# Stacking copies of q and k issued on GpSimd's queue or on SP's: one core, a macaron layer

## The chip, the cores and the metric

The kernel runs on one core of one Trainium2 chip. The metric is the device time of one execution in microseconds. The kernel before was timed three times: 2951.03, 2951.1 and 2961.06 us, median 2951.1 us.

## The reference

A layer of three parts with residual connections, on `x` of 16 sequences x 512 tokens x 128 values, float32:

```
x = x + 0.5 * ffn(layernorm(x))
x = x + attn(layernorm(x))
x = x + 0.5 * ffn(layernorm(x))
```

`ffn` routes each token to 2 of 8 experts (gate = sigmoid of the router's score) and adds a shared expert; each expert is `(silu(x W_in) * (x W_gate)) W_out`, 128 -> 256 -> 128. The change is in `attn`: 16 heads of 8 values,

```
scores = (q k^T + einsum('bhqd,qkd->bhqk', q, rel_emb[clip(i - j, -128, 128) + 128])) / sqrt(8)
local  = softmax(scores) v
global = (sigma M) / (sigma z + 1e-6),   sigma = elu(q) + 1
out    = (gate * local + (1 - gate) * global) Wo^T + bo
```

with `q, k, v = x W^T + b` and `gate = sigmoid(gate_alpha)`.

## The kernel before, in words

X stays in SBUF for the whole kernel. `ffn_phase` runs twice, `attention_phase` between them. Float32 products are made exact enough by splitting an operand into a high and a low part (`q_hi = round(q)`, `q_lo = q - q_hi`).

The attention goes over 128 items: 16 sequences x 4 sets of 4 heads (`set_of`) x 2 halves of the 512 queries (`half_of`). The program of each engine is written out as a list of slots, `for c in SLOTS: slot(c)`, one slot per item, eight (`PER`) per sequence, and each slot has four groups `k`. In slot `c` PE does the transposed scores of item `c`, the plain scores of item `c + 2` (for the row maxima), the relative products of item `c + 4` (`band_product`, L768), and parts of the preparation of the coming sequence and of the output of the leaving one. `(2, 0)` below is slot 2 of the eight, group or half 0.

The relative term takes a way through DRAM. PE multiplies the stacked queries with the table of relative embeddings into `ps_r` (L768, one buffer); ACT copies it to `src` (`at_src`, L904, `band_out_of_psum`), for which it first waits until the band write of the item before has landed and so freed that half of `src`; POOL (`send_band`) adds a column of padding (L952, L953) and writes it to `at_band` in DRAM (L959); SP (`fetch_rel`, L1027) reads it back with a skewed stride, so that the diagonals become rows, into `rel`; POOL's `fill_far` (L969) fills the part beyond distance 128. DVE then adds `rel` to the plain scores and takes the row maxima (L1089), one item ahead PE turns these (L797), DVE copies them to `mrow` (L1099), and SP copies `mrow` into a row of the stacked queries `qs` (`maxima_in`, L1036), so that the transposed scores have the maximum subtracted by the product itself. PE waits for that copy at the first group of a slot (`scores_turned`, L730).

The stacked operands `qs` and `ks` hold, for each head of a set, three parts on 24 partitions: `q_hi, q_hi, q_lo` against `k_hi, k_lo, k_hi`. Each of the 12 pieces of `qs` and of the 12 of `ks` is a copy of its own within SBUF (`spread`, L1044): 32 partitions x 2 KB onto 8 partitions x 8 KB, 64 KB. They are issued four at a time at the six places `QUERIES_IN` (2,0), (2,1), (3,0) and `KEYS_IN` (3,1), (4,0), (4,1). The queries are needed by `band_product` from (4,0) on, for the coming sequence.

On SP the order in a slot is: fetch of `rel` half 0 of item `c + 3` (four DMAs), the maxima of item `c + 1`, four stack copies where the place has them, fetch of half 1, four stack copies. On POOL: `send_band(c + 3, 1)`, `fill_far(c + 3)`, `send_band(c + 4, 0)`, then `project`: `q_lo` in slot 1, `k_lo` in slot 2 (L977, L980), three operations for sigma and the bias in slot 3 (L983, L986, L988), one in slot 4 (L993); and in slot 3 the sum of the two outputs (L1007).

Of the kernel before, what the change touches and what calls it, by code (L numbers as in the profile page):

```python
# [6 lines left out]
F32, F32R, BF16, U32 = mybir.dt.float32, mybir.dt.float32r, mybir.dt.bfloat16, mybir.dt.uint32  # L7
# [522 lines left out]
def attention_phase(nc, io, X, STATS, tables):  # L530

    D = X.shape[2]
    H, HD = io["head_of"].shape[1], io["M"].shape[1]
# [4 lines left out]
    HG = 4  # L538
    SETS = H // HG
    PART = 3  # L540
    ROW = PART * HD
    HALF = 2 * P
    PER = 2 * SETS
# [7 lines left out]
    R2 = 2  # L551
# [6 lines left out]
    QUERIES_IN = ((2, 0), (2, 1), (3, 0))  # L558
    KEYS_IN = ((3, 1), (4, 0), (4, 1))

    with ExitStack() as ctx:
# [19 lines left out]
        q_hi, q_lo = sb("q_hi", [P, S], F32R), sb("q_lo", [P, S], F32R)  # L581
        k_hi, k_lo = sb("k_hi", [P, S], F32R), sb("k_lo", [P, S], F32R)
# [72 lines left out]
        q_in = [ring(f"q_in{r}", 16 * PART * HG) for r in range(R2)]  # L655
# [20 lines left out]
        def item(c):  # L676

            return c if 0 <= c < ITEMS else None

        def coming(c):  # L680

            b = c // PER + 1
            return b if 0 <= b < B else None
# [261 lines left out]
        @block.gpsimd  # L945
        def _(pool):
            def send_band(c, l):

                j = c
                pool.wait_ge(qr_out.sem, qr_out.at(j, 2 * l + 2))  # L950
                edge = src[:, l, :, BAND - 1:BAND]
                pool.tensor_copy(far[:, c % RREL, l], edge).then_inc(pad_done.sem, 1)  # L952
                pool.tensor_copy(src[:, l, :, BAND:WIDE], edge.broadcast_to([P, HG, PAD])).then_inc(pad_done.sem, 1)  # L953
                if item(c - 2) is not None:
                    r_ring, n = rel_ring(c - 2, l)
                    pool.wait_ge(r_ring.sem, r_ring.at(n, 64))
                pool.wait_ge(pad_done.sem, pad_done.at(j, 2 * l + 2))
                heads = band.ap()[(2 * c + l) % 4].rearrange("p (h e) -> p h e", h=HG)
                pool.dma_start(heads[:, :, PAD:HEADW], src[:, l]).then_inc(band_out[l].sem, 16)  # L959

            def fill_far(c):

                j = c
                t_done.wait(pool, j, -3 * 2 * HG)
                pool.wait_ge(pad_done.sem, pad_done.at(j, 4))
                for l in range(2):
                    key = P * (2 * half_of(c) + l - 1) + WIDE + 1
                    if key < S:
                        pool.tensor_copy(rel[:, c % RREL, l, :, key:S],  # L969
                                         far[:, c % RREL, l].broadcast_to([P, HG, S - key])).then_inc(fill_done.sem, 1)  # L970

            def project(c):

                b, r, place = coming(c), 1 - par_of(c), c % PER
                if place == 1:
                    pool.wait_ge(qhi_done.sem, qhi_done.at(b, 1))
                    pool.tensor_tensor(q_lo[:], q32[:], q_hi[:].bitcast(F32), ALU.subtract).then_inc(qlo_done.sem, 1)  # L977
                elif place == 2:
                    pool.wait_ge(khi_done.sem, khi_done.at(b, 1))
                    pool.tensor_tensor(k_lo[:], k32[:], k_hi[:].bitcast(F32), ALU.subtract).then_inc(klo_done.sem, 1)  # L980
                elif place == 3:
                    g_prod.wait(pool, b, -2)
                    pool.tensor_scalar(sigma[:, r, :], q32[:], 0.0, None, ALU.min).then_inc(neg_done.sem, 1)  # L983
                    pool.wait_ge(neg_done.sem, neg_done.at(b, 1))
                    pool.wait_ge(xn_done.sem, xn_done.at(b, 1))
                    pool.tensor_scalar(q32[:], q32[:], 0.0, None, ALU.max).then_inc(pos_done.sem, 1)  # L986
                    rows = X[:, bass.ds(b * QPB, QPB), :]
                    pool.tensor_tensor(rows, rows, bo[:].rearrange("p (t d) -> p t d", t=1).broadcast_to([P, QPB, D]),  # L988
                                       ALU.add).then_inc(bo_done.sem, 1)
                elif place == 4:  # L990
                    pool.wait_ge(neg_exp.sem, neg_exp.at(b, 1))
                    pool.wait_ge(pos_done.sem, pos_done.at(b, 1))
                    pool.tensor_tensor(sigma[:, r, :], sigma[:, r, :], q32[:], ALU.add).then_inc(sigma_done.sem, 1)  # L993

            def slot(c):
                if item(c + 3) is not None:
                    send_band(c + 3, 1)
                    fill_far(c + 3)
                if item(c + 4) is not None:
                    send_band(c + 4, 0)  # L1000
                if coming(c) is not None:
                    project(c)
                if leaving(c) is not None and c % PER == 3:
                    b = leaving(c)
                    pool.wait_ge(o_step.sem, o_step.at(b, 2 * QPB))
                    pool.wait_ge(g_step.sem, g_step.at(b, 6))
                    pool.tensor_tensor(glob[:], glob[:], local[:], ALU.add).then_inc(mixed_done.sem, 1)  # L1007
            for c in SLOTS:
                slot(c)

        @block.sync
        def _(sp):
            def fetch_rel(c, l):

                j, qb = c, 2 * half_of(c) + l
                sp.wait_ge(band_out[l].sem, band_out[l].at(j, 16))
                n = j // 2
                sp.wait_ge(fill_done.sem, fill_done.at(n, l + 1 if half_of(c) == 0 else 3))
                max_done.wait(sp, j, 4 * (l + 1) - 2 * 2 * HG)
                r_ring, n = rel_ring(c, l)  # L1020
                for g in range(4):
                    first = P - 1 - 32 * g if qb == 0 else 0
                    last = BAND - 1 - 32 * g if qb == QPB - 1 else WIDE
                    key = P * (qb - 1) + 32 * g + 1 + first
                    row = ((2 * c + l) % 4 * P + 32 * g) * PITCH
                    rows = bass.AP(band, row + PAD + first, [[PITCH - 1, 32], [HEADW, HG], [1, last - first]])
                    sp.dma_start(rel[32 * g:32 * g + 32, c % RREL, l, :, key:key + last - first], rows).then_inc(r_ring.sem, 16)  # L1027

            def maxima_in(c):

                j = c
                sp.wait_ge(m_row.sem, m_row.at(j, 1))
                m_ring, n = pair_ring(m_in, c)
                at = (ROW * R2 + par_of(c)) * SETS * S + set_of(c) * S + HALF * half_of(c)
                to = bass.AP(qs[:].tensor, at, [[32 * R2 * SETS * S, HG], [1, HALF]])
                sp.dma_start(to.bitcast(F32), mrow[:, c % R2, :].bitcast(F32)).then_inc(m_ring.sem, 16)  # L1036

            def spread(c, b, n, parts, to, rings):

                r = b % R2  # L1040
                for m in range(HG * n, HG * n + HG):
                    h, a = divmod(m, PART)
                    at = 32 * h + HD * a
                    sp.dma_start(to[at:at + HD, r].bitcast(F32), parts[a][32 * h:32 * h + 32, :].bitcast(F32)).then_inc(rings[r].sem, 16)  # L1044

            def stack(c, half):

                b, place = coming(c), (c % PER, half)
                if place in QUERIES_IN:
                    n = QUERIES_IN.index(place)  # L1050
                    if n == 0:
                        sp.wait_ge(qlo_done.sem, qlo_done.at(b, 1))
                        t_done.wait(sp, c - c % PER, 0)
                    spread(c, b, n, (q_hi, q_hi, q_lo), qs, q_in)
                elif place in KEYS_IN:
                    n = KEYS_IN.index(place)
                    if n == 0:
                        sp.wait_ge(klo_done.sem, klo_done.at(b, 1))
                    spread(c, b, n, (k_hi, k_lo, k_hi), ks, k_in)

            def slot(c):
                if item(c + 3) is not None:
                    fetch_rel(c + 3, 0)
                if item(c + 1) is not None:
                    maxima_in(c + 1)
                if coming(c) is not None:
                    stack(c, 0)
                if item(c + 3) is not None:
                    fetch_rel(c + 3, 1)
                if coming(c) is not None:  # L1070
                    stack(c, 1)
            for c in SLOTS:
                slot(c)

# [332 lines left out]
```

## Time and profile before

| | |
|---|---|
| median of 3 runs | 2951.1 us |
| profiled execution, its own time | 2947.33 us |
| its span | 2945.5 us |
| TensorE clock granted, mean | 0.961 |
| PE busy | 2752.1 us (93%) |
| DVE / ACT / POOL busy | 1893.1 / 1735.6 / 1392.2 us (64 / 59 / 47%) |

Lines beginning with an engine are instructions or groups of them; `SPq` and `POOLq` are DMAs issued by SP and by GpSimd (POOL). A DMA's duration is that of its issue; its landing is separate. Busy digits are tenths of a slice of span / 40, here 73.6 us.

### The profile page before, as it was taken

What the parts mean: (1) busy time and instruction counts of PE and PEld (TensorE: products, weight loads), DVE (VectorE), ACT (ScalarE), POOL (GpSimd) and SP (SyncE); (2) the same over time, 40 slices, a digit from 0 to 9 for tenths busy, and PEclk for the clock granted to TensorE, in tenths of its full rate; (3) what the DMA queues carried; (4) which work ended last, traced back from release to release, by engine and by line L of the source; (5) the groups of instructions that cost most, each with busy time, mean ns of one, the idle gap of its engine ahead of it and who ended that gap; (6) DMA issues with size and microseconds to landing.
All of it is one profiled execution on the core that took longest, in us unless ns stands there. A gap on an engine that the chain in (4) does not pass through costs nothing. (4 is left out here: it accounts for less than half of the span.)

```text
span 2945.5 us, 60238 instructions
## 1 busy us (share of the span) xinstructions
PE 2752.1 (93%) x18624; PEld 1985.9 (67%) x18624; DVE 1893.1 (64%) x4781; ACT 1735.6 (59%) x3222; POOL 1392.2 (47%) x1728
## 2 busy tenths in 40 slices
PE   5999999999499999999999999999998999999999
PEld 4777777777255666566666565666656777777777
DVE  7666666667256666666666666666647666666665
ACT  4656566655256666556666555666646656665655
POOL 3555555555444344444434444444414555555554
PEclk9999999999689999999999999999998999999999
DMA  4000000000377788888878877887831000000000
GB/s 115 1 0 0 0 0 0 0 0 1 66 220 221 223 235 230 213 219 224 226 219 224 225 213 215 229 224 228 230 103 50 8 7 4 7 7 4 7 6 9
DMA packets 233801, 324.94 MB, mean 110 GB/s; under 512 B 29444, under 2 KB 188548, under 8 KB 233604
## 3 DMA queue, kind: packets, MB, share of 16 engines
q1 hardware_dynamic: 194436, 171.36, 24.5%
q0 software_dynamic: 36864, 150.49, 15.3%
q8 instruction: 106, 1.74, 0.3%
q10 hardware_dynamic: 2304, 0.61, 0.1%
q14 instruction: 91, 0.75, 0.1%
HBM read 141.68 MB, written 154.92 MB: 101 GB/s over the span
## 5 line engine op out<-in xcount | busy, mean ns | idle before, releaser
L1089 DVE CUSTOM_DVE_ANT_0 at_junk<-at_ps_s,at_rel 128x512 bf16<-128x512 f32 x1024 | 666.1, 688 | 403.9 <-PE at_ps_s L758 386.3
L895 ACT ACTIVATE at_probs<-at_ps_t 128x512 f32<-128x512 f32 x1024 | 558.7, 595 | 504.5 <-PE at_ps_t L743 504.3
L378 POOL TENSOR_TENSOR ffn_h_lo<-ffn_h,ffn_h_hi 128x512 fp32r<-128x512 f32 x384 | 502.1, 1311 | 475.6 <-ACT ffn_h_hi L305 475.6
L489 DVE TENSOR_TENSOR ffn_h<-ffn_silu,ffn_ps_gate 128x512 f32<-128x512 f32 x576 | 393.7, 683 | 406.7 <-ACT ffn_silu L348 404.4
L305 ACT CAST ffn_h_hi<-ffn_h 128x512 fp32r<-128x512 f32 x576 | 358.8, 623 | 408.4 <-DVE ffn_h L489 407.0
L194 PE MATMUL ffn_ps_mid<-ffn_xT_hi,ffn_w_mid 128*128 128x512 f32 x1152 | 480.2, 417 | 22.7 <-DVE ffn_h L489 11.5
L743 PE MATMUL at_ps_t<-tab_ident,at_rel 128*128 128x128 f32 x3328 | 497.1, 290 | 0.0
L194 PE MATMUL ffn_ps_gate<-ffn_xT_hi,ffn_w_gate 128*128 128x512 f32 x1152 | 456.7, 396 | 0.0
L194 PE MATMUL ffn_ps_out<-ffn_h_hi,ffn_w_out 128*128 128x512 f32 x1152 | 453.9, 395 | 0.2
L743 PEld LDWEIGHTS at_ps_t<-tab_ident,at_rel 128*128 128x128 f32 x3328 | 372.2, 146 | 82.3 <-issue 22.7
L348 ACT ACTIVATE ffn_silu<-ffn_ps_mid 128x512 f32<-128x512 f32 x576 | 343.8, 597 | 80.2 <-PE ffn_ps_gate L194 73.2
L372 POOL TENSOR_TENSOR ffn_xe<-ffn_xn,ffn_gate 128x512 f32<-128x512 f32 x256 | 269.3, 1057 | 238.6 <-DVE ffn_gate L451 124.4
L730 PEld LDWEIGHTS at_ps_t<-at_qs,at_ks 25*128 25x128 f32 x2048 | 189.7, 188 | 281.7 <-ACT at_probs L895 126.4
L730 PE MATMUL at_ps_t<-at_qs,at_ks 25*128 25x256 f32 x2048 | 300.7, 335 | 55.3 <-DMA at_qs<-at_mrow 55.0
L904 ACT COPY at_src<-at_ps_r 128x512 f32<-128x512 f32 x512 | 304.3, 594 | 65.0 <-PE at_ps_r L768 38.2
L783 PE MATMUL at_ps_v<-at_probs,at_v 128*32 128x256 f32 x4096 | 337.8, 403 | 0.2 <-ACT at_probs L895 0.2
L952 POOL COPY at_far<-at_src 128x4 f32<-128x4 f32 x256 | 48.2, 188 | 606.2 <-ACT at_src L904 603.7
L768 PE MATMUL at_ps_r<-tab_rs,at_qs 128*128 128x512 f32 x512 | 260.6, 509 | 36.6 <-DMA at_qs<-at_q_lo 22.0
L758 PE MATMUL at_ps_s<-at_ks,at_qs 24*128 24x512 f32 x1024 | 278.6, 512 | 0.5 <-DVE at_mx L1089 0.3
L194 PEld LDWEIGHTS ffn_ps_mid<-ffn_xT_hi,ffn_w_mid 128*128 128x128 f32 x1152 | 217.6, 189 | 83.0 <-DVE ffn_h L489 18.2
L194 PEld LDWEIGHTS ffn_ps_gate<-ffn_xT_hi,ffn_w_gate 128*128 128x128 f32 x1152 | 217.0, 188 | 52.6
L959 POOL DMA_DIRECT2D at_band<-at_src x256 | 184.0, 719 | 144.5 <-POOL at_src L953 133.7
(161 smaller groups left out, 4000.2 us busy)
## 6 DMA issues: line engine op xcount, KB each, us to landing
at_band<-at_src POOLq DMA_DIRECT2D x256, 574.0 KB, 4.8
at_rel<-at_band SPq DMA_DIRECT2D x512, 143.5 KB, 3.8
at_qs<-at_q_hi SPq DMA_DIRECT2D x128, 64.0 KB
at_ks<-at_k_hi SPq DMA_DIRECT2D x128, 64.0 KB
at_rel<-at_band SPq DMA_DIRECT2D x64, 128.0 KB, 3.5
at_rel<-at_band SPq DMA_DIRECT2D x64, 127.5 KB, 3.1
at_rel<-at_band SPq DMA_DIRECT2D x64, 112.0 KB, 2.9
at_rel<-at_band SPq DMA_DIRECT2D x64, 111.5 KB, 3.5
```

The costliest lines, as they stand in the source:

```text
L194: ins = pe.matmul(out, lhs(a), rhs(b), start=start and i == 0, stop=stop and i == 2)
L305: act.copy(h_hi[:, u % RH, :], h[:, u % RH, :]).then_inc(hhi_done.sem, 1)
L348: act.activation(silu[:, u % RH, :], ps_mid[:, u % 2, :], ACT.Silu).then_inc(silu_done.sem, 1)
L378: pool.tensor_tensor(h_lo[:, u % RH, :], h[:, u % RH, :], h_hi[:, u % RH, :].bitcast(F32), ALU.subtract).then_inc(hlo_pool.sem, 1)
L489: dve.tensor_tensor(h[:, u % RH, :], silu[:, u % RH, :], ps_gate[:, u % 2, :], ALU.mult).then_inc(h_done.sem, 1)
L730: pe.matmul(ps_t[:, i, HALF * n:HALF * (n + 1)], ks[rows, r, s, kb * P:(kb + 1) * P], q, start=(n == 0), stop=False, skip_group_check=True)
L743: ins = pe.matmul(ps_t[:, i, HALF * n + P * l:HALF * n + P * (l + 1)], rel[:, c % RREL, l, 2 * hp + i, kb * P:(kb + 1) * P], ident[:], sta ...
L758: pe.matmul(ps_s[:, i, :], qs[rows, r, s, rows_of(c, l)], ks[rows, r, s, :], start=True, stop=True).then_inc(s_done.sem, 1)
L783: ins = pe.matmul(ps_v[32 * g:32 * g + 32, 0:HALF], v[:, r, kb, at:at + 32], probs[:, kb // 2, g, kb % 2, :], start=(kb == 0), stop=(kb == ...
L895: act.activation(probs[:, kp, 2 * hp + i].rearrange("p n q -> p (n q)"), ps_t[:, i, :], ACT.Exp).then_inc(exp_done.sem, 1)
L904: act.copy(src[:, l, 2 * hp:2 * hp + 2, 0:BAND], ps_r[:].rearrange("p (h t) -> p h t", h=2)).then_inc(qr_out.sem, 1)
L1089: dve.tensor_tensor_reduce(out=junk[:, i, :], in0=ps_s[:, i, :], in1=rel[:, c % RREL, l, h, :], scale=1.0, scalar=-3e38, op0=ALU.add, op1= ...
```

## The change

`spread` and `stack` move from SP's program to POOL's, with their waits, and issue on `pool` instead of `sp`. On POOL `stack(c, 0)` stands between `fill_far(c + 3)` and `send_band(c + 4, 0)`, and `stack(c, 1)` between `send_band(c + 4, 0)` and `project(c)`. Data, places, order among themselves and semaphores of the copies stay as they are.

```diff
@@ POOL
+            def spread(c, b, n, parts, to, rings):
+                r = b % R2
+                for m in range(HG * n, HG * n + HG):
+                    h, a = divmod(m, PART)
+                    at = 32 * h + HD * a
+                    pool.dma_start(to[at:at + HD, r].bitcast(F32), parts[a][32 * h:32 * h + 32, :].bitcast(F32)).then_inc(rings[r].sem, 16)
+
+            def stack(c, half):
+                b, place = coming(c), (c % PER, half)
+                if place in QUERIES_IN:
+                    n = QUERIES_IN.index(place)
+                    if n == 0:
+                        pool.wait_ge(qlo_done.sem, qlo_done.at(b, 1))
+                        t_done.wait(pool, c - c % PER, 0)
+                    spread(c, b, n, (q_hi, q_hi, q_lo), qs, q_in)
+                elif place in KEYS_IN:
+                    n = KEYS_IN.index(place)
+                    if n == 0:
+                        pool.wait_ge(klo_done.sem, klo_done.at(b, 1))
+                    spread(c, b, n, (k_hi, k_lo, k_hi), ks, k_in)
+
             def slot(c):
                 if item(c + 3) is not None:
                     send_band(c + 3, 1)
                     fill_far(c + 3)
+                if coming(c) is not None:
+                    stack(c, 0)
                 if item(c + 4) is not None:
                     send_band(c + 4, 0)
                 if coming(c) is not None:
+                    stack(c, 1)
                     project(c)
@@ SP: the same spread and stack, on sp, removed; and
             def slot(c):
                 if item(c + 3) is not None:
                     fetch_rel(c + 3, 0)
                 if item(c + 1) is not None:
                     maxima_in(c + 1)
-                if coming(c) is not None:
-                    stack(c, 0)
                 if item(c + 3) is not None:
                     fetch_rel(c + 3, 1)
-                if coming(c) is not None:
-                    stack(c, 1)
```

## Rows read from the trace of the kernel before

**Rows 1.** The page: busy tenths of 40 slices of the span.

```profile
PE   5999999999499999999999999999998999999999
...
DMA  4000000000377788888878877887831000000000
```

**Rows 2.** Waits, 860 to 2100 us: engine, line, awaited; us, times, longest.

```profile
POOL at_far L952 <- ACT at_src L904: 533.7, 194, 7.5
...
PE at_ps_t L730 <- DMA at_qs<-at_mrow: 53.8, 22, 3.3
...
ACT at_src L904 <- DMA at_band<-at_src: 14.0, 17, 1.6
...
PE at_ps_r L768 <- DMA at_qs<-at_q_lo: 11.3, 14, 1.7
```

**Rows 3.** Timeline, PE, slots 3 to 5: start, us, instruction, [idle before].

```profile
1472.55 0.39 PE L730 MATMUL at_ps_t<-at_qs,at_ks 25*128 25x256 f32 x2 [3.30 <-DMA at_qs<-at_mrow]
...
1475.76 0.80 PE L768 MATMUL at_ps_r<-tab_rs,at_qs 128*128 128x512 f32 x1 [1.68 <-DMA at_qs<-at_q_lo]
...
1485.43 0.48 PE L768 MATMUL at_ps_r<-tab_rs,at_qs 128*128 128x512 f32 x1
...
1495.24 0.48 PE L768 MATMUL at_ps_r<-tab_rs,at_qs 128*128 128x512 f32 x1
```

**Rows 4.** Stretches of 10 us: busy per engine, granted clock, DMA share, GB/s.

```profile
1460.00:1470.00 10.00, 9.25 (x89) 5.63 (x85) 6.55 (x21) 6.76 (x14) 8.15 (x11) 1.00 1.01 215
1470.00:1480.00 10.00, 5.77 (x38) 3.92 (x38) 2.62 (x8) 2.27 (x4) 3.51 (x6) 0.70 0.92 229
```

**Rows 5.** DMA issues by line, 860 to 2100 us (min/median/max ns), and SP's timeline.

```profile
L1036 SPq DMA_DIRECT2D at_qs<-at_mrow x115: 533/554/1050, 865.2 to 2099.1; - x115
...
L1044 SPq DMA_DIRECT2D at_qs<-at_q_hi x117: 671/677/1413, 859.7 to 2076.9; - x117
...
L1027 SPq DMA_DIRECT2D at_rel<-at_band x916: 302/432/2320, 863.3 to 2098.6; - x184
...
DMA to landing us min/median/max: 2.3/3.6/7.2
...
L959 POOL DMA_DIRECT2D at_band<-at_src x230: 711/711/782, 859.9 to 2099.6; - x115
...
DMA to landing us min/median/max: 3.8/4.8/7.9
...
1466.30 0.57 SPq L1036 DMA_DIRECT2D at_qs<-at_mrow  x1
```

**Rows 6.** Timeline, POOL, slots 2 to 5.

```profile
1451.16 0.59 POOL L969 COPY at_rel<-at_far 128x384 f32<-128x384 f32 x1
1455.40 0.19 POOL L952 COPY at_far<-at_src 128x4 f32<-128x4 f32 x1 [3.66 <-ACT at_src L904]
...
1457.03 1.36 POOL L980 TENSOR_TENSOR at_k_lo<-at_k,at_k_hi 128x512 fp32r<-128x512 f32 x1
1460.55 0.19 POOL L952 COPY at_far<-at_src 128x4 f32<-128x4 f32 x1 [2.16 <-ACT at_src L904]
...
1461.51 0.73 POOL L959 DMA_DIRECT2D at_band<-at_src  x1 [0.54 <-POOL at_src L953]
1462.17 2.31 POOL L969 COPY at_rel<-at_far 128x1408 f32<-128x1408 f32 x2
1464.61 0.19 POOL L952 COPY at_far<-at_src 128x4 f32<-128x4 f32 x1
...
1466.24 1.60 POOL L983 TENSOR_SCALAR at_sigma<-at_q 128x512 f32<-128x512 f32 x1
...
1472.77 0.77 POOL L959 DMA_DIRECT2D at_band<-at_src  x1 [0.56 <-POOL at_src L953]
...
1481.37 0.19 POOL L952 COPY at_far<-at_src 128x4 f32<-128x4 f32 x1 [7.31 <-ACT at_src L904]
```

**Rows 7.** Timeline, ACT, slot 3.

```profile
1467.54 0.59 ACT L904 COPY at_src<-at_ps_r 128x512 f32<-128x512 f32 x1 [0.92 <-DMA at_band<-at_src]
```

More of the change, by code:

```diff
@@ L1036, in maxima_in @@
                 sp.dma_start(to.bitcast(F32), mrow[:, c % R2, :].bitcast(F32)).then_inc(m_ring.sem, 16)
[L1038 to L1059, printed above, removed]
             def slot(c):
```

## The prediction

> **What bounds the kernel now.** I read the page's slices first. The two outer stretches are the feed-forward phases, which the change does not touch; the middle, some 750 to 2200 us, is the attention, where the DMA row rises to 7 to 8 tenths while PE stays at 9 [rows 1]. So there PE is the engine to follow, with the DMA engines close behind. The list of waits of 14 sequences says what stops PE: it waits for the maxima row (at_mrow) 22 times, 53.8 us in all, and for the last stacked query part 14 times, 11.3 us; together 65.1 us, or 4.65 us per sequence. POOL's largest wait, 533.7 us, is for ACT's copies of the relative products, so POOL runs level with PE and ACT and can't run ahead; ACT itself waited for band writes to land 17 times, 14.0 us [rows 2].
>
> One sequence, in order of time, shows where. PE idles 3.30 us, to 1472.55, for the maxima row, works, idles 1.68 us for the stacked queries, and then runs at the lower clock: the product of 512 columns at 1475.76 takes 0.80 us where the ones at 1485.43 and 1495.24 take 0.48 [rows 3]. The 10 us around it have a granted clock of 0.70 and 5.77 us of PE work, against 1.00 and 9.25 in the 10 us before [rows 4]. With two levels, 1.2 and 2.4 GHz, a mean of 0.70 over 10 us means 6 us at the lower one; by the product at 1475.76 they begin there and, less some idle gaps, hold about 4.8 us of work at half speed. So I put the loss at 2.4 us, and the stop costs 3.3 + 1.7 + 2.4 = 7.4 us of the 86.6 us that a sequence lasts (115 maxima DMAs from 865.2 to 2099.1 us, 10.82 us apart, eight per sequence [rows 5]). Without it this product of slot 4, group 3, would be at 1485.43 - 7.4 = 1478.0.
>
> Why it stops: the maxima DMA issued at 1466.30 is waited for until 1472.55, 6.2 us, behind eight stack DMAs and four fetches on the same queue [rows 3, 5], while the DMA engines have a share of 1.01 [rows 4].
>
> **Part 1, what leaves SP.** 24 issues of 0.671 to 0.68 us leave it, 16.2 us per sequence [rows 5]. The maxima DMA is not issued much earlier, since the fetch ahead of it waits for POOL's fill (L969 at 1462.17 [rows 6]); but no stack data lies ahead of it. Taken at the 3.6 us in which fetches land [rows 5], it is there at about 1470.4, not 1472.55, and the idle of 3.3 us falls to some 1 us. The last query DMA leaves at about 1467.7 (part 2) instead of 1470 or so, and its idle of 1.7 us goes too. Alone, this part is worth up to the 7.4 us per sequence: 15 sequences are stacked inside the steady stretch, so up to 111 us.
>
> **Part 2, what POOL takes on.** Each stack DMA costs POOL an issue. POOL has issued no such copy, so its cost is bounded: the SP queue's shortest fetch is 0.302 us, its stack DMA 0.671; POOL's own band write has a minimum and a median of 0.711, and its next instruction starts 0.66 us after the start (1461.51 to 1462.17) [rows 5, 6]. Ends: 0.3 and 1.0 us, the latter being POOL's 0.66 and half as much again for a copy whose two sides have different partition counts (on SP that kind costs 0.67 against 0.43 for a fetch, half as much again too [rows 5]). I take POOL's own row, 0.66 per DMA, 2.64 for four.
>
> Now POOL's order with this added, by the starts in [rows 6]:
> - Slot 2. The fill ends at 1451.75, the first four end at 1454.4; POOL was idle until 1455.40, so they cost nothing. The next four stand ahead of k_lo (1457.03), which then ends at 1461.0; the idle of 2.16 us hides all but 0.45.
> - Slot 3. Band write and fill take from 1460.55 to 1464.61, 4.06 us: 1465.1. Four DMAs: 1467.7. The other band write, 1.63 us: 1469.3. Four more: 1472.0. Then sigma, the maximum, the bias, the sum of the outputs and the padding, from 1466.24 to the issue at 1472.77, 6.53 us. So the first band write of slot 4 is issued at 1478.5: 5.7 us late.
> - Slot 4. The short fill (0.59) ends at 1479.8, four DMAs at 1482.4, a band write at 1484.0, four more at 1486.6, the last part of sigma (taken as k_lo's 1.36) at 1488.0; the padding ahead of the next band write takes 1.0 (1460.55 to 1461.51), so that is issued at 1489.0. Most of it goes into the idle of 7.31 us.
>
> **Part 3, who waits for POOL.** The band write frees one half of at_src; ACT's copy of the next product into that half waits for it, queued behind it on ACT are the exponentials, and PE's next product waits for the copy (ps_r has one buffer). The write lands 4.8 us after its issue in the median; the one of 1461.51 held ACT until 1467.54, 6.0 us [rows 5, 6, 7]. I take 5.4: 1478.5 + 5.4 = 1483.9, ACT's copy 0.6 [rows 7], PE's product of slot 4, group 3, at 1484.6. Unhindered it would be at 1478.0, and before it was at 1485.43 [rows 3]. So PE stops here 6.6 us, instead of 5.0 us and a slow stretch. An idle of this length is followed by the lower clock, as the 5.0 us were, and that costs another 2.4 us (as above); it was already over at 1485.43 before, and is not yet begun at 1484.6 now. The product of slot 5, group 3, follows 9.8 us after [rows 3]: 1484.6 + 9.8 + 2.4 = 1496.8 against 1495.24. The write at 1489.0 lands at 1494.4, in time. The other waits: the wait for q_lo and k_lo is for POOL's own work, finished earlier; the fetches behind fill and band write (issued 1479.8, landing in about 5.4) reach DVE at 1485, before its need, at that pace; the four query DMAs directly ahead of a band write in POOL's queue are 256 KB, 1.1 us at 229 GB/s [rows 4], and delay only the write issued near 1468.6, whose copy has some 2 us of room.
>
> **Sum.** +1.6 us per sequence, 15 sequences: +24 us. The first sequence's stack stands before any product and takes 24 issues either way: 0. The profiled execution took 2947.3 us for a span of 2945.5, 0.13% under the median of 2951.1. So 2971 us on its scale and 2975 us against the median.
>
> The sum is steep in one number: 12 DMAs stand between the 0.45 us of lateness and the write that decides, so 0.1 us more or less per DMA is 1.2 us per sequence, 18 us in all. At 0.3 us per DMA the product is at 1480.3; with half the clock loss, -3.9 us per sequence, -58 us. At 1.0 us: +4.1 us more, +86 us.
>
> **Rivals.** *A, the stop goes.* If POOL takes 0.3 to 0.4 us per copy, or the band writes land in 4.8 us or less once SP's queue is emptier, PE's wait of 4.65 us falls by more than what POOL adds: -25 to -70 us, 2880 to 2925. For it: SP's row of maxima is the late one [rows 2]; against it: POOL has not that much idle time in slot 3, none at all behind 1462.17. The Trainium skill ("Perfetto Trace Analysis", DMA Optimizations) advises to balance issues over the engines that can issue when descriptor generation is the bottleneck; the trace agrees that SP is late, but in slot 3 it shows POOL full too.
>
> *B, slower by much.* POOL's cost per copy is nearer 0.9 to 1.0, or the landing is 6 us and more: +60 to +86 us, 3010 to 3040. It decides from about 0.8 us on. For it: a saturated DMA and a copy of unequal sides; against it: 230 writes at 0.711 with hardly any spread.
>
> *C, even.* The two stops balance, within 0.5% (14.8 us, about what a measurement can tell from no change): that is at 0.45 (-2.5 us, so -0.9 per sequence) to 0.6 us (-0.7, so +0.9) per copy.
>
> *D, POOL's issues are held by DVE.* If each of them waited for one DVE instruction of the 0.68 us kind, 1.35 us per copy would be +8.3 us more per sequence, near 3100. Against it: the band writes keep 0.711 us, maximum 0.782, though DVE is busy for 6.55 of 10 us in such a stretch [rows 4, 5]. The Trainium skill ("SBUF — State Buffer", two separate sides) states that GpSimd can't write its descriptors while DVE runs a two-port operation such as an fp32 copy within SBUF; the only such copy in the loop is k_hi, once per sequence, so by that rule the sum hardly changes.
>
> **Chances.** The forecast with its own range of +8 to +50 us has 0.47, A 0.24, B 0.16, C 0.10, D 0.03. Slower by over 0.5%: 0.40 of the forecast's, B and D, 0.59; within: 0.07 and C, 0.17; faster: A, 0.24. The range leaves out the ends of A, and D with the end of B: 2915 to 3035.
>
> **What would show it.** Right: a POOL DMA of at_qs and at_ks near 0.7 us; ACT waiting for DMA at_band in slot 4 by several us per sequence; PE's wait for at_mrow under 1 us per sequence and a new one of L768 for ACT at_src; slower clock after it. Wrong: POOL copies under 0.5 us or over 0.9, a POOL wait for at_src that stays above 300 us, or PE still waiting for the maxima row.

## The result, and the profile after

The changed kernel takes 2982.68 us (median of 6 runs, 2973.88 to 2988.33) against 2948.66 us for the kernel before (6 runs): +34 us, a ratio of 1.0109 with a 95% interval of 1.0085 to 1.0134. The forecast was 2975 us, +24 us. Direction and range held; several of the steps behind them did not, as shown below. The profiled execution took 2988.33 us for a span of 2986.5.

The waits after, in the stretch of [rows 2] (engine, line, awaited: us in all, times, longest):

```profile
PE at_ps_t L730 <- DMA at_qs<-at_mrow: 59.7, 36, 4.7
PE at_ps_r L768 <- ACT at_src L904: 30.1, 36, 1.8
PE at_misc_e L853 <- POOL at_glob L1033: 2.3, 3, 1.0
...
ACT at_src L904 <- DMA at_band<-at_src: 64.4, 52, 2.4
SPq L25 <- POOL at_rel L969: 584.6, 110, 10.2
```

ACT waits for band writes 64.4 us instead of 14.0, and PE for ACT's copies 30.1 us, as forecast. PE's wait for the last query copy (11.3 us before) is gone. But its wait for the maxima row has not gone: 59.7 us in 36 pieces, where it was 53.8 in 22. POOL's wait for ACT's copies is 376.9 us, where it was 533.7. SP waits 584.6 us for POOL's fill, which was 292.8 us before; most of that growth is no lateness of POOL, since 16.2 us of issues per sequence have left SP, some 227 us in 14 sequences, and SP comes to the fill earlier by them.

The new POOL issues (minimum, median, maximum in ns), a form of L1001 for the keys and one for the queries, the landing of all L1001 copies, and then the band write with its own:

```profile
L1001 POOL DMA_DIRECT2D at_ks<-at_k_hi x120: 544/569/615, 865.6 to 2129.8; - x120
L1001 POOL DMA_DIRECT2D at_qs<-at_q_hi x114: 544/577/649, 862.0 to 2111.6; - x114
...
DMA to landing us min/median/max: 3.3/6.2/9.0
...
L959 POOL DMA_DIRECT2D at_band<-at_src x229: 711/732/816, 864.9 to 2139.7; - x115
...
DMA to landing us min/median/max: 3.9/4.9/9.0
```

A copy costs POOL 0.57 us. One sequence, to be laid beside the one of [rows 3, 6] (in order it is the one before that, but its slots hold the same work): its turn of the maxima, L797, in slot 2 is at 1383.05, in the kernel before at 1454.25, so 71.2 us are added to compare. POOL, the last band write of slot 3, then from the end of that slot:

```profile
1396.41 0.76 POOL L959 DMA_DIRECT2D at_band<-at_src  x1 [0.58 <-POOL at_src L953]
...
1403.63 1.26 POOL L1033 TENSOR_TENSOR at_glob<-at_glob,at_local 128x512 f32<-128x512 f32 x1
1404.85 0.18 POOL L952 COPY at_far<-at_src 128x4 f32<-128x4 f32 x1
...
1405.85 0.81 POOL L959 DMA_DIRECT2D at_band<-at_src  x1 [0.59 <-POOL at_src L953]
1406.62 0.56 POOL L969 COPY at_rel<-at_far 128x384 f32<-128x384 f32 x1
```

SP in the same slot, issues only:

```profile
1394.38 0.54 SPq L1062 DMA_DIRECT2D at_qs<-at_mrow  x1
1395.55 13.86 SPq L1053 DMA_DIRECT2D at_rel<-at_band  x8
1409.45 0.53 SPq L1062 DMA_DIRECT2D at_qs<-at_mrow  x1
```

And PE:

```profile
1400.21 0.39 PE L730 MATMUL at_ps_t<-at_qs,at_ks 25*128 25x256 f32 x2 [1.63 <-DMA at_qs<-at_mrow]
...
1405.58 0.27 PE L797 MATMUL at_misc_p<-tab_ident,at_mx 128*128 128x128 f32 x1
...
1411.03 0.51 PE L768 MATMUL at_ps_r<-tab_rs,at_qs 128*128 128x512 f32 x1 [0.38 <-ACT at_src L904]
1415.97 0.58 PE L730 MATMUL at_ps_t<-at_qs,at_ks 25*128 25x256 f32 x2 [2.73 <-DMA at_qs<-at_mrow]
1417.05 0.78 PE L768 MATMUL at_ps_r<-tab_rs,at_qs 128*128 128x512 f32 x1
...
1427.05 0.48 PE L768 MATMUL at_ps_r<-tab_rs,at_qs 128*128 128x512 f32 x1
```

ACT's copies of the relative products that waited for a band write:

```profile
1404.07 0.59 ACT L904 COPY at_src<-at_ps_r 128x512 f32<-128x512 f32 x1 [1.58 <-DMA at_band<-at_src]
...
1410.39 0.59 ACT L904 COPY at_src<-at_ps_r 128x512 f32<-128x512 f32 x1 [1.32 <-DMA at_band<-at_src]
```

The turn of slot 4 and the row behind it in the kernel before:

```profile
1480.43 0.41 PE L797 MATMUL at_misc_p<-tab_ident,at_mx 128*128 128x128 f32 x1
...
1481.19 0.57 SPq L1036 DMA_DIRECT2D at_qs<-at_mrow  x1
```

The late band write of slot 4 is issued at 1405.85 (1477.05 on the time of before, where it was 1472.77). The fill follows at 1406.62 and ends at 1407.18; only then does SP issue the four fetches that wait for it (the eight issues merged in the row run to 1409.41), and behind them the maxima row at 1409.45, 3.9 us after PE turned the maxima at 1405.58. In the kernel before that took 0.8 us in slot 4 (1480.43 to 1481.19); it was in slot 3 that it took long, 3.2 us (1463.13 to 1466.30), and there it now takes 1.2 us (1393.14 to 1394.38). The row is needed at 1413.2, when PE's work before it ends, and is there at 1415.97. The row of slot 3 is waited for too, 1.63 us at 1400.21. The product of slot 4, group 3, at 1411.03 corresponds to 1482.2, 3.2 us earlier than before; the one of slot 5, group 3, at 1427.05 to 1498.25, 3.0 us later than before. From the one to the other it is 16.0 us, where it was 9.8. Between them lie the new wait for the row and the lower clock behind it (0.78 us per product again). PE's idle time for ACT at the product of 1411.03 is 0.38 us. The band write of 1396.41, with four query copies issued just ahead of it, landed 7.6 us after its issue, and ACT's copy at 1404.07 waited for it 1.58 us.

The same holds over the steady stretch (14 sequences before, 13 after). Between the turn of slot 3 and that of slot 4 PE waited for the row 39.9 us in 14 pieces before, and 15.3 us in 11 after; between those of slots 4 and 5 not at all before, and 32.2 us in 13 after. SP issues the row of slot 4 4.2 us after its turn in the median (0.8 before), that of slot 3 1.2 us (3.7 before). So the stop of one slot has moved to the next, and a smaller one is left behind. The stretches (PE, PEld, DVE, ACT, POOL busy, granted clock, DMA share, GB/s):

```profile
1390.00:1400.00 10.00, 8.01 (x78) 4.66 (x77) 6.70 (x21) 6.28 (x12) 9.06 (x15) 1.00 1.05 222
1400.00:1410.00 10.00, 9.79 (x84) 6.65 (x85) 4.97 (x15) 4.96 (x9) 8.99 (x14) 0.83 0.70 200
1410.00:1420.00 10.00, 6.89 (x49) 4.03 (x47) 4.23 (x14) 4.22 (x8) 7.52 (x11) 0.77 1.09 190
1420.00:1430.00 10.00, 10.00 (x76) 5.98 (x79) 5.35 (x17) 5.49 (x11) 2.09 (x6) 0.72 0.82 220
```

The DMA engines are full in two of the four stretches, as in [rows 4], and the clock is below 1.00 in three. Three sequences follow each other at 88.3, 88.4 and 89.1 us, against 86.9, 87.1 and 85.6 before (the turns of slot 2: 1206.35, 1294.67, 1383.05, 1472.11 against 1194.68, 1281.53, 1368.64, 1454.25), 2.1 us more on average. Over 13 sequences in a row these turns go from 939.30 to 2100.30, against 939.05 to 2061.64: 3.0 us more per sequence, 38.4 of the 41.0 us between the two profiled executions. The one profiled after is the slowest of its six; the 34 us between the medians are 2.3 us for each of 15 sequences.

### The profile page after: what moved, and what is told of

It is laid out like the page before. It is cut to its first block and busy times, and to the rows that moved or that the text cites. A ratio compares the mean times of both kernels' runs of the same rounds, so it can differ in the third digit from the quotient of the medians.

```text
span 2986.5 us, 60238 instructions
## 1 busy us (share of the span) xinstructions
PE 2766.2 (93%) x18624; PEld 1981.8 (66%) x18624; DVE 1897.9 (64%) x4781; ACT 1736.3 (58%) x3222; POOL 1597.3 (53%) x2112
## 3 DMA queue, kind: packets, MB, share of 16 engines
q0 software_dynamic: 55296, 175.73, 19.8%
## 5 line engine op out<-in xcount | busy, mean ns | idle before, releaser
L783 PE MATMUL at_ps_v<-at_probs,at_v 128*32 128x256 f32 x4096 | 345.4, 411 | 0.2 <-ACT at_probs L895 0.2
```

Of the source, the lines that this page charges most:

```text
L783: ins = pe.matmul(ps_v[32 * g:32 * g + 32, 0:HALF], v[:, r, kb, at:at + 32], probs[:, kb // 2, g, kb % 2, :], start=(kb == 0), stop=(kb == ...
```

## The experiments

Each ratio is against the kernel before, run beside it on the same chip, with its 95% interval. Two theories at the start: L, POOL is late by the time that its copies take, and ACT and SP wait for it; D, the copies' data, moved to POOL's queue, delays the band writes.

**1 and 2. The maxima row ahead of the fetch, with the copies on POOL and on SP.**

```diff
             def slot(c):
+                if item(c + 1) is not None:
+                    maxima_in(c + 1)
                 if item(c + 3) is not None:
                     fetch_rel(c + 3, 0)
-                if item(c + 1) is not None:
-                    maxima_in(c + 1)
```

> The changed kernel with one exchange on SP: the maxima row of item c + 1 is issued ahead of the fetch of half 0 of item c + 3, so that it no longer stands behind a fetch that waits for POOL's fill. Theory L (POOL is late by its copies, and SP's fetch, waiting for POOL's fill, holds the maxima row behind it): PE's wait for at_mrow, 63.7 us in 860 to 2140 us, falls under 25 us, and 20 to 50 us of time go with it (2935 to 2960 us); ACT's wait for band writes stays near 69 us or grows. Theory D (the data of the copies in POOL's queue delays the band writes): the maxima row gains little, under 10 us, as PE then waits for ACT instead.

> The kernel before with the same exchange on SP. Both theories: PE's wait for at_mrow (53.8 us) falls, as the row is ahead of a fetch of half 0; in slot 3 it still stands behind the eight copies of slot 2, which SP ends only at 1464.4 us, so half of the wait may stay. -10 to -35 us against before (2915 to 2940 us). If it is as fast as the same exchange with the copies on POOL, or faster, POOL's queue brings nothing of its own.

Measured: 3034.52 us, 1.0311 (1.0285 to 1.0336), and 3051.35 us, 1.0376 (1.0347 to 1.0406). Both far slower, so the expectations missed in size and sign. PE's wait for the row did vanish (none with the copies on POOL, 0.7 us with them on SP), but SP now waits for DVE's row, 5.7 us at a time on average with the copies on POOL (616.8 us, 108 times) and 4.9 with them on SP, and the fetch behind it is late for DVE. The waits with the copies on SP:

```profile
ACT at_probs L895 <- PE at_ps_t L743: 485.4, 455, 3.1
...
SPq L1036 <- DVE at_mrow L1099: 407.9, 83, 7.2
...
DVE at_junk L1089 <- DMA at_rel<-at_band: 216.2, 105, 4.1
```

So in most slots SP's old order is the better one; whether it is the worse one where POOL is late, these runs can't show. These two show the price of a late fetch; they don't measure how much of the change's loss goes through SP's order.

**3 and 4. An eighth of the data, on POOL and on SP.**

```diff
-                    pool.dma_start(to[at:at + HD, r].bitcast(F32), parts[a][32 * h:32 * h + 32, :].bitcast(F32)).then_inc(rings[r].sem, 16)
+                    pool.dma_start(to[at:at + HD, r, :, 0:S // 8].bitcast(F32), parts[a][32 * h:32 * h + 32, 0:S // 8].bitcast(F32)).then_inc(rings[r].sem, 16)
```

(and the same line on `sp`). Both kernels leave out seven eighths of `qs` and `ks`, and serve only to take the data away.

> The changed kernel with 64 of 512 columns copied in each of the 24 copies (an eighth of the data, so 7/8 of qs and ks are left out). POOL's 24 issues stay, near 0.56 us each. Theory L: POOL is late by issue time, so the difference to the same cut with the copies on SP stays near +34 us. Theory D: the difference goes to within 10 us, since hardly any data stands ahead of the band writes.

> The kernel before with 64 of 512 columns copied in each of the 24 copies (7/8 of qs and ks left out). SP's 24 issues stay near 0.67 us. If the maxima row was late by the data ahead of it on SP's queue, PE's wait for it falls under 20 us and the time by 30 to 80 us; if by SP's issue time, both stay within 15 us of before.

Measured: 2931.72 us, 0.9959 (0.9942 to 0.9975), and 2913.65 us, 0.9909 (0.9878 to 0.9939). The difference between the two queues is 18 us, where it is 34 us with all data: between the +34 of L and the 10 of D. On POOL the row is hardly waited for any more, and PE waits for POOL's work (the sum of the outputs, L1033) instead:

```profile
PE at_misc_e L853 <- POOL at_glob L1033: 27.1, 14, 2.3
PE at_ps_r L768 <- ACT at_src L904: 16.6, 22, 2.5
PE at_ps_t L730 <- DMA at_qs<-at_mrow: 12.7, 11, 2.5
```

In one sequence of this run SP issues the row of slot 4 at 1380.37, 6.8 us after its turn at 1373.54 (6.7 in the median of the sequences), so later than the 3.9 us above; PE comes to it at 1384.88 and finds it there. It landed within 4.5 us, where it took 6.5 with all the data. PE came later too: it had waited 1.99 us for POOL, and the clock was lower (0.88 from 1370 to 1380). So in this run the row's late issue no longer stops PE, by a quicker landing and a later PE together.

On SP the wait for the row stays (59.4 us, 40 times) though the data is gone; PE's wait for the last query copy is gone, and the time falls by 31 us against the runs beside it. The time falls as if the data had been the reason, and the wait stays as if it had not, so the expectation is met by neither side. So before, the row's wait is not removed by taking data away, while in the changed kernel most of it is (59.7 to 12.7 us).

**5. POOL's time without the data.** The kernel before, and on POOL at the six places, called where the change calls `stack`:

```diff
+            def occupy(c, half):
+                if (c % PER, half) in QUERIES_IN + KEYS_IN:
+                    for m in range(3):
+                        n = coming(c) * 18 + (QUERIES_IN + KEYS_IN).index((c % PER, half)) * 3 + m
+                        if n > 0:
+                            pool.wait_ge(spared.sem, n)
+                        pool.memset(spare[:], 0.0).then_inc(spared.sem, 1)
```

> The kernel before, its 24 copies on SP, and on POOL at the six places of the change three memsets of 560 bf16 values each into a tile that nothing reads (each waits for the last one): some 2.2 us of POOL's time per place, as four copies took, and no DMA. Theory L (POOL's time): PE waits for ACT's copies and SP waits for the fill as in the changed kernel; +25 to +80 us against before. Theory D (the copies' data on POOL's queue): within 10 us of before.

Measured: 2954.82 us, 1.0049 (1.0029 to 1.0068), +9 us. Each memset takes 0.564 us, three of them with their waits 1.9 us of POOL's time (four copies: 2.2). This is below what L said and at the edge of D: POOL's time added here costs something, a quarter (by the medians) to under a half (by the ratios) of the change's loss. But it does not cost it the way L says. PE waits for ACT's copies 1.1 us in all (1.2 before, 30.1 in the changed kernel), ACT for band writes 13.2 us, SP for the fill 271.4 us: none has grown. PE's wait for the row is 38.0 us and that for the last query copy 32.2, which are 53.8 and 11.3 before. SP's copies still stop PE at the start of slot 4, and while PE stands POOL catches up: in one sequence the first band write of slot 4 goes out 4.5 us ahead of that slot's turn (1222.77 and 1227.26), where it is 7.7 us ahead before and 0.3 us behind in the changed kernel. So the test does not measure L's chain.

**6 and 7. One half of the copies on POOL.** `stack` on POOL has the branch of the queries (or of the keys) alone, and SP keeps the other branch at its places:

```diff
 @@ POOL                                  @@ SP
-   elif place in KEYS_IN: ...            +   if place in KEYS_IN: ...     (queries on POOL)
-   if place in QUERIES_IN: ...           +   if place in QUERIES_IN: ...  (keys on POOL)
```

> Only the 12 query copies are issued on POOL, at their places; the 12 key copies stay on SP. Theory L: POOL has 3.66 and 2.16 us idle in slot 2 for the first eight, and in slot 3 only one place of four stands before the sigma work, so POOL is late by some 2.5 us in slot 4, less than the room there; SP is free ahead of the row of slot 3. -20 to +5 us against before, faster than the full move by 30 us or more. Theory D: the query copies are the ones ahead of the band writes of slot 3, so half of the change's loss or more stays: +10 to +35 us.

> Only the 12 key copies are issued on POOL; the queries stay on SP. Theory L: the first four stand ahead of the sigma work of slot 3, the others in slot 4, and POOL is late by 2.2 us at the first write of slot 4 and 4 to 6 us behind; the query copies still stand ahead of the row of slot 3 on SP, so that wait stays: 0 to +30 us against before. Theory D: 0 to +20 us. It tells mainly, together with the other half, which half carries the loss.

Measured: queries on POOL 2947.17 us, 1.0010 (0.9993 to 1.0028), no change, where L had said -20 to +5 us and D +10 to +35; keys on POOL 2993.18 us, 1.0177 (1.0152 to 1.0202), +47 us and more than the whole move. The loss appears only when the keys move. Both theories had put the keys' half at +30 us or less. The trace with the keys on POOL shows why it is more. PE, then POOL, then SP:

```profile
1406.53 0.80 PE L768 MATMUL at_ps_r<-tab_rs,at_qs 128*128 128x512 f32 x1 [6.84 <-DMA at_qs<-at_q_lo]
```

```profile
1394.94 0.65 POOL L1001 DMA_DIRECT2D at_ks<-at_k_hi  x1
1395.52 0.63 POOL L1001 DMA_DIRECT2D at_ks<-at_k_lo  x1
1396.08 1.13 POOL L1001 DMA_DIRECT2D at_ks<-at_k_hi  x2
1397.19 1.57 POOL L983 TENSOR_SCALAR at_sigma<-at_q 128x512 f32<-128x512 f32 x1
```

```profile
1394.26 0.57 SPq L1056 DMA_DIRECT2D at_qs<-at_mrow  x1
...
1397.50 0.75 SPq L1064 DMA_DIRECT2D at_qs<-at_q_lo  x1
```

The last query copy is issued at 1397.50 and waited for until 1406.53: 9 us from issue to use, beside four key copies that POOL issued between 1394.94 and 1397.19. With all copies on SP the last query copy left at some 1469.6 and PE had it at 1475.76, 6.2 us, the keys standing behind it in program order. PE waits 52.3 us for query copies in this kernel (14 times), 11.3 before. From issue to use the last query copy takes 7.9 to 9.0 us in 13 of 15 sequences (5.1 and 5.9 in the other two), 3.1 to 6.4 us before, and 3.1 to 6.7 us with the memsets, where POOL's time is taken and no key data moved. The keys are not needed for two more slots; on a second queue they go out beside what is needed now. That it is their data that makes the query copy late is the reading that fits all three kernels.

**8. The keys one place later, all on POOL.**

```diff
-    KEYS_IN = ((3, 1), (4, 0), (4, 1))
+    KEYS_IN = ((4, 0), (4, 1), (5, 0))
```

> The changed kernel with the key copies one place later each: (4,0), (4,1), (5,0) instead of (3,1), (4,0), (4,1). POOL then has only four copies in slot 3, where the sigma work is, and four in slot 5, where it was idle. Theory L: the first band write and the fill of slot 4 come 2.2 us earlier, so 15 to 35 us are won against the changed kernel (2945 to 2968 us). Theory D: the same data ahead of the same number of band writes, within 8 us of the changed kernel.

Measured: 2961.96 us, 1.0070 (1.0047 to 1.0093): 21 us less than the changed kernel by the medians, inside L's range, but 0.4% (some 11 us) by the ratios, whose intervals overlap, so between what L and D say. It frees slot 3 both of 2.2 us of POOL's time and of 256 KB, so it does not tell the two apart. Nor did the waits that L names fall: PE waits 59.0 us for the row and 32.9 for ACT's copies, ACT 71.8 us for band writes.

**9 and 10. The maxima row issued by ACT.** `maxima_in` goes from SP's slot to ACT's, on `act`:

```diff
+                    if k == 2 and item(c + 1) is not None:
+                        maxima_in(c + 1)
```

> The kernel before with the DMA of the maxima row issued by ACT, at group 2 of the slot, right after DVE has the row, instead of by SP behind the fetch of half 0. It costs ACT one issue of some 0.55 us per slot. If the row was late because of what stood ahead of it on SP's queue (issues or data), PE's wait for it (53.8 us) falls under 10 us; the wait for the last query copy (11.3 us) stays or grows, since the copies now end it alone. -20 to -60 us against before (2885 to 2925 us).

> The changed kernel with the same row issued by ACT. Theory L (POOL late, its fill late, SP's fetch waits for the fill and holds the row): PE's wait for the row, 59.7 us in 860 to 2100 us, falls under 10 us, and what is left is PE's wait for ACT, which waits for POOL's band writes; the difference to the same kernel with the copies on SP is then the price of POOL's lateness through the band writes alone, +15 to +45 us. Theory D (the engines are full and the row lands late wherever it is issued): the wait stays above 35 us, and both kernels with the row on ACT gain less than 15 us.

Measured: 3064.25 us, 1.0402 (1.0360 to 1.0445), and 3134.15 us, 1.0638 (1.0596 to 1.0681). Both expectations missed. The waits with the copies on SP:

```profile
PE at_ps_t L730 <- DMA at_qs<-at_mrow: 152.4, 94, 3.3
```

PE waits in 94 of some 106 slots. ACT issues the row at 1204.30 and 1214.66, 2.6 and 2.9 us after the turns at 1201.72 and 1211.78, since an exponential and its wait stand ahead of it, where SP needs 0.6 us in slot 2. So in an ordinary slot the row has less than 2 us to spare, and the test measures a later row, not a freed one. It shows how sharp the deadline is that SP's late row meets in slot 5 (3.9 us after the turn instead of 0.8). With the copies on POOL as well PE waits 174.5 us, 87 times. It does not settle theory D, as its expectation had hoped.

**11 and 12. The keys later on SP, and with the queries on POOL.** The edit of experiment 8 on the kernel before and on that of experiment 6.

> The kernel before with the key copies one place later each, (4,0), (4,1), (5,0). The same edit won some 20 us on the changed kernel. If that came from POOL's time in slot 3, nothing is won here: within 8 us of before. If it came from the copies' data meeting the last queries and the row, it wins here too: -8 to -25 us.

> Queries on POOL, keys on SP one place later each: the half of the move that cost nothing, with the keys out of slot 3. If what is left of PE's wait for the row there (59.3 us) comes from the keys' issues or data on SP's queue in slots 3 and 4, -10 to -30 us against before; if from POOL's late fill, within 8 us.

Measured: 3021.17 us, 1.0259 (1.0218 to 1.0299), and 2998.65 us, 1.0176 (1.0135 to 1.0217). Outside both expectations: on SP the third group of keys now ends too late for the plain scores of the next sequence.

```profile
PE at_ps_t L730 <- DMA at_qs<-at_mrow: 49.8, 22, 3.3
PE at_ps_s L758 <- DMA at_ks<-at_k_hi: 43.2, 14, 3.9
```

That new wait of 3.1 us per sequence and its clock (0.92 over the stretch, 0.95 before) hide whatever the edit may win in slot 3, so the question it was made for stays open. With the queries on POOL the new wait is 23.8 us (14 times), and the second run leaves its question open for the same reason. Of the ten kernels that copy all the data none beats the kernel before; queries on POOL equals it.

## Why the prediction was right, and where it was not

- *A POOL issue of 0.66 us.* 0.57 us. By the forecast's own rule (12 copies) that is 1.1 us less per sequence, so only +0.5.
- *POOL late by 5.7 us at the first band write of slot 4.* 4.3 us (1405.85, or 1477.05, against 1472.77); with 0.57 instead of 0.66 the same addition gives 4.6. This step was right, its price too high.
- *ACT and PE wait for that write, and PE stops 6.6 us for it.* The wait is there and the stop is not: the write was there 4.5 us after its issue (1405.85 to 1410.39, ACT's copy), not 5.4, PE's product came at 1482.2, not at 1484.6, and PE stood idle before it for 0.38 us, since it was late itself by the row of slot 3 and the clock. All of PE's waits for ACT's copies are 30.1 us, some 2.2 us per sequence. ACT's wait is 64.4 us, 50 us more, and in the sequence shown more than half of it is for another write, that of 1396.41, which took 7.6 us to land; the forecast gave it 1.1 us for the query copies ahead of it and some 2 us of room.
- *PE's wait for the row falls under 1 us per sequence.* This step failed: 59.7 us in some 14 sequences, 4.3 us each. Two things were left out. The forecast followed POOL's late fill to SP's fetch and to DVE, and found it in time, but not to the row that stands behind that fetch on SP (1409.45 instead of about 1406.2). And it took the row at a landing of 3.6 us because no stack data was ahead of it on its own queue; the DMA engines had a share of 1.05 and 1.09 in two of the stretches, and from issue to use it took 5.8 us in slot 3 (1394.38 to 1400.21) and 6.5 in slot 4 (1409.45 to 1415.97), as before (6.2).
- *The clock falls once more, 2.4 us.* Right in kind, too small: 0.83, 0.77 and 0.72 over 30 us are, worked out as the forecast did, 13.6 us at the lower level, where the kernel before had 6.8 (0.70 and 0.96). PE falls to it twice, behind 1.63 us idle at 1400.21 and 2.73 us at 1415.97.
- *Sum.* +1.6 us per sequence forecast, 2.3 by the medians and 3.0 in the profiled executions measured. With the measured 0.57 us per copy and 4.5 us of landing the forecast's own sum is -0.4 us per sequence, -6 us in all. The rest of the measured loss, the wait for the row in slot 5 and the longer low clock, is not in that sum, and the two errors offset each other. That POOL's lateness reaches PE through those who wait for POOL was right; by which path and for how much was not, and that the time fell into the range was largely luck.
- *Its own signs of being wrong.* Two of them came: PE still waits for the maxima row, and POOL's wait for `at_src` is 376.9 us, above the 300 that it named.
- *Rival A* (the stop goes) failed because the stop moved from slots 3 and 4 to slots 4 and 5. Its condition that the band writes land in 4.8 us or less did hold for the write that was to decide. *C* had its condition met, a copy at 0.45 to 0.6 us, and yet the two kernels are not within 0.5%, for the same missing wait. *D* failed: 0.649 us at most for a copy. The Trainium skill's rule on two-port DVE work ("SBUF — State Buffer", two separate sides) is neither needed nor disproved here. *B* did not hold: a copy costs less than 0.9 us, and the time is +34 us, not +60.

What carries the loss: the queries alone on POOL cost nothing, and the keys added to them make the loss (experiment 6 and the change). The traces show who waits for whom (POOL's fill, SP's fetch, the row, PE, in all 13 sequences), and the thin copies that about half of the difference between the queues goes when the data goes (+34 to +18 us). How the rest divides is not shown: memsets of nearly the same length cost +9 us, but by other waits than those of the change. That the keys' data beside the query copies makes them late is what experiment 7 shows for its kernel, beside the kernel before and the memsets; in the changed kernel itself, where the queries leave before the keys on the same queue, that it is the data that makes the row land late is argued from experiment 3, where the row left later still and landed sooner, and PE's wait fell from 59.7 to 12.7 us; a later PE has its part in that fall.

## What to carry to other kernels

When issues are moved from a queue that is late to an engine that is not, follow the receiving engine's lateness to everybody who waits for it, and from each of them to what is queued behind: here POOL's fill, SP's fetch, and behind it the row that PE waits for. One queue is also an order of importance: in this kernel the key copies stayed behind the urgent query copies only as long as they shared a queue. Before a small transfer is moved, measure its slack in an ordinary slot; here it was some 2 us or less, and two rearrangements that looked harmless, each tried on both kernels, cost 3 to 6%.

## What the runs showed of the hardware

- POOL's issue of a 64 KB copy within SBUF, 32 partitions onto 8, takes 0.57 us, less than its 574 KB write to DRAM (0.71 to 0.73) and less than the same copy on SP's queue (0.67).
- POOL's copies count more packets: its queue has 55296 packets after and 36864 before, 18432 more for 384 copies, 48 each; SP's has 15360 fewer, 40 each.
- An eighth of the columns left POOL's issue at 0.574 us and the copies of q_hi landed in 3.6 us in the median, where it was 5.7.
